# A fused eight-layer kernel without its setup block: the loads move into the first attention

## The chip, the cores and the metric

The kernel runs on one core of a Trainium2 chip as one program. The metric is the device time of a run in microseconds. Engines in the text: TensorE (PE, matrix products), VectorE (DVE), ScalarE (ACT), GpSimd (POOL) and SyncE (SP). SP issues most transfers, ScalarE some; each of the two has a queue of its own, and both queues are served by the core's 16 DMA engines.

## The reference, cut to what matters

The input is `x`, 128 sequences of 64 rows by 128 columns in float32, with a context of 128 x 64 x 96. Eight layers are added onto x: four cross attentions, each followed by a feed-forward part. Each addition is scaled by the tanh of a learned gate. Only the first two layers and the weights derived ahead of time concern the change:

```python
# layer 0: cross attention of 8 heads of 64, masked, over the context
x = x + tanh(g_xattn[0]) * (attention(layernorm(x), ctx, mask) @ W_o + b_o)
# layer 1: experts weighted by a router, around one causal attention
logits = normalize(h) @ normalize(sim_matrix, axis 0) - sigmoid(gates)
# derived ahead of time from inputs:
#  sim / |sim| per column, sigmoid(gates), tanh of the 8 gates, bias rows * tanh(gate)
#  layer 3's 128 x 128 matrix from w_freq (a Fourier transform there and back)
#  layer 6's null key and value, multiplied into W_q and W_out
```

## The kernel before, in words

`x` (64 tiles of 128 rows) stays in the on-chip memory throughout, and so do all weights of the first layers. `program` (L2463) runs `setup`, then one block after another, each with a program for every engine; between blocks stands a barrier (L2498 to L2500).

`setup` (L81) is a block of its own. SP issues 28 small loads (L181), all counted on one semaphore, `ld_small`. ScalarE issues x (4 MB, L188) and then 17 larger loads (L190). TensorE, VectorE and ScalarE each wait for all 28 small loads before their first instruction, and SP waits at the end for everything. Then the derived weights are computed: VectorE squares the router's matrix, TensorE sums the columns with a matrix of ones (L213), GpSimd takes the power -1/2 (L205); the Fourier matrices go through four products, two copies and two more (L216 to L229); the null values are 16 small products (L224); VectorE scales `l3_wq`, multiplies it by the null key and reduces it (L242 to L247), and scales six bias rows by their gates (L257).

`wide_attention` (L393) is layer 0. It works in 16 units of 4 tiles of 128 rows. Products in float32 are made of three passes over high and low parts (`product3`, L348 to L350). Each tile's step on TensorE is: transposes of the probabilities (L746), the projection of the tile before (L682), attend (L672), the scores of two tiles on (L660), for t = 1 the transposes of the normalised rows of two units on (`turn`, L620), then value, key and query jobs for later tiles. VectorE has the mask and scale (L903), the maximum (L907), the subtraction (L915), the sum and reciprocal (L921, L923), the norm's moments (L296, L301) and its scaling (L310), and the addition to x (L929). GpSimd has the norm's 1/sqrt (`rstd`, L318, L320), the multiplication of the probabilities (`scale_probs`, L549; "probs" in the prediction), the split of the context (L524, L526) and its spreading (L539, L540), and the bias (L325). ScalarE copies out of the accumulators and takes the exponential.

Ahead of the loop each engine has a written-out head, in which the first unit's keys, queries and the scores of tiles 0 and 1 are made. On GpSimd the head ends with `scale_probs(0)` and the bias of groups 0 and 1; the loop begins with `scale_probs(1)`, the split of the third unit's context and the `rstd` of the third group, then `scale_probs(2)`:

```python
scale_probs(0, first, 0)
if not null:
    norm.bias(pool, 0), norm.bias(pool, 1)
```

`gated_attention` (L2033) is layer 1. Its head on TensorE is `turn(0), router(0, 0), turn_gates(0, 0), turn(1), router(1, 1)`; between the router and `turn_gates` VectorE runs a chain of some 25 tiny instructions (L2326 to L2384), with one exponential on ScalarE in it (`gate_exp`, L2268). The gates are then written to memory, and SP loads them back spread over all partitions (L2088).

Of the kernel before, what the change touches and what calls it, by code (L numbers as in the profile page):

```python
# [12 lines left out]
P = 128  # L13
# [67 lines left out]
def setup(c, d):  # L81
# [3 lines left out]
    names = []  # L85
# [33 lines left out]
    for n in ("l3_wq", "l3_wk", "l3_wv"):  # L119
# [25 lines left out]
    c.open_work(26 * 1024)  # L145
    scr = c.work[:, 0:9 * 512].rearrange("p (n w) -> p n w", w=512)
    dftc, dfts, wr, wi = (scr[:, i, 0:D] for i in range(4))
    a1, a2, cn, sn = (scr[:, 4 + i, 0:D] for i in range(4))
    nsc = scr[:, 8, 0:D]
    simsq = c.work[:, 15 * 512:15 * 512 + 16]  # L150
    simn2 = c.work[:, 15 * 512 + 16:15 * 512 + 32]
    ones = c.work[:, 15 * 512 + 128:15 * 512 + 256]
    nprod = c.work[:, 16 * 512:18 * 512].rearrange("p (h k) -> p h k", k=DH)

    loads_small, loads_x, loads_big = [], [], []
    loads_small += [(c.w["ident"][:, :], d["ident"]), (c.w["tg"][:, :], d["gates"]), (c.w["rows"][:, :, :], d["rows"]),
                    (c.w["hm4"][:, :], d["hm4"]), (c.w["nkrow"][:, :], d["nkrow"]), (c.w["nvsel"][:, :, :, :], d["nvsel"]),
                    (c.w["nvcol"][:, :], d["nvcol"]), (c.w["gncol"][:, :], d["gncol"]), (c.w["l2_bcol"][:, :], d["l2_bcol"]),
                    (c.w["l3f_b1"][:, :], d["l3f_b1"]),
                    (dftc, d["dftc"]), (dfts, d["dfts"]), (wr, d["wr"]), (wi, d["wi"]),  # L160
                    (c.w["l3f_u1"][:, :], d["l3f_u1"]), (c.w["l3f_v1"][:, :], d["l3f_v1"]),
                    (c.w["l3f_u2"][:, :, :], d["l3f_u2"]), (c.w["l3f_v2"][:, :], d["l3f_v2"]),
                    (c.w["dup"][:, :], d["dup"]), (c.w["l0f_sim"][:, :], d["sim"]), (c.w["l0f_sig"][:, :], d["gates0"]),
                    (c.w["causal"][:, :], d["causal"]), (c.w["iota16"][:, :], d["iota16"]),
                    (c.w["l2f_wr"][:, :], d["l2f_wr"]), (c.w["l2f_bias"][:, :], d["l2f_bias"]), (c.w["tri4"][:, :, :], d["tri4"]),
                    (c.w["l3_wq"], d["l3_wq"]), (c.w["l3_wo"], d["l3_wo"])]
    for n in ("l0_wq", "l0_wk", "l0_wv", "l0_wo"):
        loads_big.append((c.w[n], d[n]))
    loads_big.append((c.ctx01[0:DC, :, :].rearrange("p a b -> p (a b)"), d["ctxT"][:, 0:2 * GT]))
    loads_big += [(c.w["l0f_w"], d["l0f_w"]), (c.w["l0f_o"], d["l0f_o"])]  # L170
    for n in ("l1_wq", "l1_wk", "l1_wv", "l1_wo", "l2_wq", "l2_wk", "l2_wvz", "l2_wo", "l3_wk", "l3_wv"):
        loads_big.append((c.w[n], d[n]))

    ld_small, ld_x, ld_big = c.sem("ld_small"), c.sem("ld_x"), c.sem("ld_big")
    xv = d["x"].rearrange("(n p) c -> p n c", p=P)
    consts, chain, pe, evac, ppow, vchain = (c.sem("su_" + n) for n in ("consts", "act", "pe", "evac", "pow", "dve"))
    with nc.Block() as block:
        @block.sync
        def _(sp):
            for dst, src in loads_small:  # L180
                sp.dma_start(dst, src).then_inc(ld_small, 16)  # L181
            sp.wait_ge(ld_small, 16 * len(loads_small))
            sp.wait_ge(ld_x, 16)
            sp.wait_ge(ld_big, 16 * len(loads_big))

        @block.scalar
        def _(act):
            act.dma_start(c.w["x"][:, :, :], xv).then_inc(ld_x, 16)  # L188
            for dst, src in loads_big:
                act.dma_start(dst, src).then_inc(ld_big, 16)  # L190
            act.wait_ge(ld_small, 16 * len(loads_small))

            A.activation(c.w["tg"][:, :], c.w["tg"][:, :], ACT.Tanh).then_inc(chain, 1)
            A.activation(c.w["l0f_sig"][:, :], c.w["l0f_sig"][:, :], ACT.Exp, scale=-1.0).then_inc(chain, 1)

        @block.gpsimd
        def _(pool):
            G.memset(ones, 1.0).then_inc(consts, 1)
            G.memset(c.w["half"][:, :], -0.5).then_inc(consts, 1)
            G.memset(c.zero[:, :], 0.0)  # L200
            G.memset(c.w["eps"][:, :], LN_EPS)

            pool.wait_ge(consts, 2)
            pool.wait_ge(vchain, 2)
            G.tensor_tensor(simn2, simn2, c.w["half"][:, :], ALU.pow).then_inc(ppow, 1)  # L205

        @block.tensor
        def _(te):
            te.wait_ge(ld_small, 16 * len(loads_small))
            te.wait_ge(vchain, 1)  # L210
            te.wait_ge(consts, 1)
            pa, pb = c.ps[:, 0, :], c.ps[:, 1, :]
            T.matmul(c.ps[:, 6, 0:16], ones, simsq, start=True, stop=True).then_inc(pe, 1)  # L213

            te.wait_ge(evac, 1)
            T.matmul(pa[:, 0:D], wr, dftc, start=True, stop=False)  # L216
            T.matmul(pa[:, 0:D], wi, dfts, start=False, stop=True)
            T.matmul(pb[:, 0:D], wr, dfts, start=True, stop=False)
            T.matmul(pb[:, 0:D], wi, nsc, start=False, stop=True).then_inc(pe, 1)

            te.wait_ge(evac, 2)
            for j in range(8):
                for b in range(2):
                    last = T.matmul(c.ps[0:16, 4, b * D:(b + 1) * D], c.w["nvsel"][:, j, b, :], c.w["l3_wo"][:, j, :],  # L224
                                    start=(j == 0 and b == 0), stop=(j == 7), skip_group_check=True)
            last.then_inc(pe, 1)
            te.wait_ge(evac, 4)
            T.matmul(c.ps[:, 5, 0:D], a1, cn, start=True, stop=False)
            T.matmul(c.ps[:, 5, 0:D], a2, sn, start=False, stop=True).then_inc(pe, 1)  # L229

        @block.vector
        def _(ve):
            ve.wait_ge(ld_small, 16 * len(loads_small))
            V.tensor_tensor(simsq, c.w["l0f_sim"][:, :], c.w["l0f_sim"][:, :], ALU.mult).then_inc(vchain, 1)
            V.tensor_scalar(nsc, dftc, -1.0, None, ALU.mult).then_inc(evac, 1)
            V.tensor_scalar(c.w["nvsel"][:, :, :, :], c.w["nvsel"][:, :, :, :], c.w["nvcol"][:, 0:1], None, ALU.mult).then_inc(evac, 1)
            V.tensor_scalar(cn, dftc, 1.0 / D, None, ALU.mult).then_inc(evac, 1)
            V.tensor_scalar(sn, dfts, 1.0 / D, None, ALU.mult)
            ve.wait_ge(pe, 1)
            V.tensor_scalar(simn2, c.ps[:, 6, 0:16], 1e-24, None, ALU.max).then_inc(vchain, 1)  # L240

            V.tensor_scalar(c.w["l3_wq"], c.w["l3_wq"], c.w["gncol"][:, 0:1], None, ALU.mult).then_inc(vchain, 1)  # L242
            ve.wait_ge(vchain, 3)
            heads = c.w["l3_wq"].rearrange("p (h k) -> p h k", k=DH)
            V.tensor_tensor(nprod, heads, bc(c.w["nkrow"][:, :], 1, 2 * HP), ALU.mult).then_inc(vchain, 1)
            ve.wait_ge(vchain, 4)
            V.tensor_reduce(c.w["l3_wnull"][:, :], nprod, AX.X, ALU.add)  # L247
            ve.wait_ge(ppow, 1)
            V.tensor_tensor(c.w["l0f_sim"][:, :], c.w["l0f_sim"][:, :], simn2, ALU.mult)
            ve.wait_ge(chain, 2)  # L250

            V.tensor_scalar(c.w["l0f_sig"][:, :], c.w["l0f_sig"][:, :], 1.0, None, ALU.add).then_inc(vchain, 1)
            ve.wait_ge(vchain, 5)
            V.reciprocal(c.w["l0f_sig"][:, :], c.w["l0f_sig"][:, :])

            for row, gate in ((0, 0), (1, 1), (2, 5), (3, 2), (4, 7), (5, 3)):
                V.tensor_scalar(c.w["rows"][:, row, :], c.w["rows"][:, row, :], c.w["tg"][:, gate:gate + 1], None, ALU.mult)  # L257
            ve.wait_ge(pe, 2)
            V.tensor_copy(a1, c.ps[:, 0, 0:D])
            V.tensor_copy(a2, c.ps[:, 1, 0:D]).then_inc(evac, 1)  # L260
            ve.wait_ge(pe, 3)
            for b in range(2):
                V.tensor_copy(c.w["l3_nwo"][:, b, :], c.ps[0:16, 4, b * D:(b + 1) * D])
            ve.wait_ge(pe, 4)
            V.tensor_copy(c.w["l1f_g"][:, :], c.ps[:, 5, 0:D])

class Norm:

# [122 lines left out]
def wide_attention(c, d, layer):  # L393

    nc = c.nc
# [95 lines left out]
    with nc.Block() as block:  # L495
# [395 lines left out]
        def _(ve):  # L891
# [84 lines left out]
            if null:  # L976
                norm.scale(ve, 1, 1)
# [1609 lines left out]
```

## Time and profile before

| | us |
|---|---|
| median of 3 runs | 3279.08 (3277.92 to 3280.07) |
| the profiled execution | 3276.91 |
| its span, first to last instruction | 3275.1 |
| TensorE busy | 3015.4 (92%) |
| VectorE busy | 2212.9 (68%) |
| ScalarE busy | 1564.1 (48%) |
| GpSimd busy | 1206.4 (37%) |
| mean granted TensorE clock | 0.969 |

The busy time of an engine is the time in which it ran an instruction. The profiled execution lies 2.2 us under the median of the runs. Times in the rows below are from the start of the span.

### The profile page before, as it was taken

To read this page: it belongs to the slowest core of one execution; us is meant where nothing else is said; L and a number is where in the kernel's file an instruction comes from. 1 tells how busy PE (TensorE), PEld (TensorE's weight loads), DVE (VectorE), ACT (ScalarE), POOL (GpSimd) and SP (SyncE) were. 2 spreads that over 40 slices of the span, in tenths; PEclk is the share of its full clock that TensorE was granted. 3 is DMA by queue.
4 is the path that set the end of the run, shared out by engine and by line. 5 is a ranking of instruction groups with operands and counts; after the bars stand their busy time and mean duration, and the time that the engine had idled before them with its cause. 6 is when DMAs were issued, how large, how long until landed. Compare 5 with 4: busy or idle time off the path is not lost. (4 is left out here: it accounts for less than half of the span.)

```text
span 3275.1 us, 90989 instructions
## 1 busy us (share of the span) xinstructions
PE 3015.4 (92%) x35250; PEld 2295.4 (70%) x35250; DVE 2212.9 (68%) x6060; ACT 1564.1 (48%) x2876; POOL 1206.4 (37%) x1408
## 2 busy tenths in 40 slices
PE   3999879999997999969997999999988999999978
PEld 2888735555555788846766888888876888888864
DVE  3677656566664555568776777777767777777755
ACT  1777611111112677636664333333335666666646
POOL 3666410000001766565441000000005766766643
PEclk8999989999998999979998999999999999999989
DMA  5000046665562000011111333333320000000001
GB/s 156 12 10 10 4 132 191 184 176 159 168 193 64 12 10 10 3 47 24 26 24 51 103 102 103 102 102 101 104 81 9 9 9 10 10 7 10 10 1 52
DMA packets 109623, 212.02 MB, mean 65 GB/s; under 512 B 18736, under 2 KB 28912, under 8 KB 108944
## 3 DMA queue, kind: packets, MB, share of 16 engines
q1 hardware_dynamic: 105232, 200.32, 21.0%
q10 hardware_dynamic: 4224, 9.59, 1.0%
q8 instruction: 91, 1.49, 0.2%
q14 instruction: 76, 0.62, 0.1%
HBM read 198.31 MB, written 5.77 MB: 62 GB/s over the span
## 5 line engine op out<-in xcount | busy, mean ns | idle before, releaser
L348 PE MATMUL ps<-parts 128*128 128x512 f32 (+2 forms) x1568 | 640.7, 409 | 46.4 <-DVE parts L953 27.6
L349 PE MATMUL ps<-parts 128*128 128x512 f32 (+2 forms) x1568 | 565.8, 361 | 0.0
L350 PE MATMUL ps<-parts 128*128 128x512 f32 (+2 forms) x1568 | 563.0, 359 | 0.0
L318 POOL TENSOR_TENSOR rstd<-mv,eps 128x4 f32<-128x4 f32 x112 | 23.8, 213 | 1223.4 <-DVE mv L301 1223.4
L348 PEld LDWEIGHTS ps<-parts 128*128 128x128 f32 (+1 forms) x1568 | 299.1, 191 | 184.9 <-ACT work L804 99.8
L1852 ACT ACTIVATE work<-ps 128x512 f32<-128x512 f32 x272 | 162.5, 597 | 453.5 <-PE ps L350 453.4
L549 POOL TENSOR_TENSOR work<-work 128x512 f32<-128x512 f32 x256 | 267.0, 1043 | 194.5 <-DVE work L923 192.6
L350 PEld LDWEIGHTS ps<-parts 128*128 128x128 f32 (+1 forms) x1568 | 298.9, 191 | 46.1
L349 PEld LDWEIGHTS ps<-parts 128*128 128x128 f32 (+1 forms) x1568 | 300.9, 192 | 13.5
L1818 PEld LDWEIGHTS ps<-early,work 128*128 128x128 f32 x2176 | 281.7, 191 | 29.8 <-DVE work L1909 11.4
L1818 PE MATMUL ps<-early,work 128*128 128x128 f32 x2176 | 289.4, 276 | 8.2 <-DVE x L2016 8.1
L1899 DVE TENSOR_TENSOR work<-work,ps 128x512 f32<-128x512 f32 x272 | 185.8, 683 | 134.2 <-PE ps L1818 120.9
L921 DVE TENSOR_REDUCE work<-work 128x8 f32<-128x512 f32 (+1 forms) x256 | 174.9, 683 | 143.5 <-ACT work L821 143.5
L2170 PE MATMUL ps<-work,early 128*128 128x512 f32 x512 | 249.4, 610 | 12.1 <-DVE work L2391 12.1
L903 DVE SCALAR_TENSOR_TENSOR ps<-ps,work 128x512 f32<-128x512 f32 x192 | 133.9, 697 | 164.6 <-PE ps L660 155.4
L804 ACT ACTIVATE work<-ps 128x512 f32<-128x512 f32 x256 | 152.8, 597 | 173.7 <-PE ps L350 170.7
L863 ACT ACTIVATE work<-ps 128x512 f32<-128x512 f32 x256 | 152.9, 597 | 133.7 <-PE ps L672 132.6
L907 DVE TENSOR_REDUCE work<-ps 128x8 f32<-128x512 f32 x256 | 176.5, 689 | 51.6 <-PE ps L660 45.0
L672 PE MATMUL ps<-work 64*64 64x64 f32 x8192 | 179.1, 225 | 20.1 <-ACT work L854 19.8
L821 ACT ACTIVATE work<-work 128x512 f32<-128x512 f32 (+1 forms) x256 | 161.9, 632 | 54.1 <-DVE work L915 52.1
L1909 DVE TENSOR_TENSOR work<-work 128x512 f32<-128x512 f32 x256 | 177.2, 692 | 15.2 <-DMA work<-expert_rows 2.6
L672 PEld LDWEIGHTS ps<-work 64*64 64x64 f32 x8192 | 145.5, 135 | 55.8 <-issue 33.6
(311 smaller groups left out, 6205.4 us busy)
## 6 DMA issues: line engine op xcount, KB each, us to landing
work<-gate_rows SPq DMA_DIRECT2D x128, 512.0 KB, 5.5
work<-expert_rows SPq DMA_DIRECT2D x512, 128.0 KB, 2.9
work<-gate_rows SPq DMA_DIRECT2D x128, 256.0 KB, 7.7
work<-in_ctxT SPq DMA_DIRECT2D x72, 192.0 KB, 2.4
out<-x SPq DMA_DIRECT2D x16, 256.0 KB, 2.3
work<-work SPq DMA_DIRECT2D x224, 16.0 KB
work<-work SPq DMA_DIRECT2D x16, 128.0 KB, 2.7
early<-in_l0f_w ACTq DMA_DIRECT2D x1, 1536.0 KB, 11.9
```

Of the source, the lines that this page charges most:

```text
L348: T.matmul(out, lh, rh, start=True, stop=False)
L349: T.matmul(out, lh, rl, start=False, stop=False)
L350: return T.matmul(out, ll, rh, start=False, stop=True)
L549: G.tensor_tensor(pn[t % 2], pr[t % 2][:, :, 0:S], bc(rec[t % 2], 2, S), ALU.mult).then_inc(p_ready, 1)
L672: last = T.matmul(ps_o[e * DH:e * DH + DH, b, j, :], vp[t % 2][rows, e, j, :], ptT[rows, j, b * S:b * S + S], start=True, stop=True)
L907: V.tensor_reduce(mx[t % 2], ps_s, AX.X, ALU.max).then_inc(max_ready, 1)
L921: V.tensor_reduce(den[t % 2], pr[t % 2], AX.X, ALU.add).then_inc(sum_ready, 1)
L1818: last = T.matmul(acc[:, t * D:(t + 1) * D], aT[b][:, t * P:(t + 1) * P], c.w["l2f_d"][:, j, :], start=(j == 0 and t == 0), stop=(j == NB ...
L1852: A.activation(sg[b], ps_g[b], ACT.Silu).then_inc(silu_ready, 1)
L1899: out = V.tensor_tensor(aT[b], sg[b], ps_u[b], ALU.mult)
L1909: V.tensor_tensor(aT[b], aT[b], wb[j % WR], ALU.mult).then_inc(a_ready, 1)
L2170: T.matmul(ps_q[u], c.w["l0f_w"][:, at:at + P], hw[p % NHW][:, e, :], start=(p == 0 and e == 0), stop=(p == NP - 1 and e == 1))
```

## The change

`setup` now only places the tensors and makes an object `Boot`, whose methods are called from the programs of layer 0's engines; there is no setup block any more. Each load has a semaphore of its own or one of a small group. The Fourier matrices come as one host-made array `dft` of five (cos, sin, -cos, cos/128, sin/128), loaded at the start of layer 1 into a buffer that is used later there, and `wri` holds the two frequency weights.

```diff
+    def sync_first(self, sp):       # SP's queue, ahead of the mask and the third context
+        sp.dma_start(*self.rows_of(0, TG)).then_inc(self.x0, 16)
+        sp.dma_start(c.ctx01[0:DC, :, :]..., d["ctxT"][:, 0:2 * GT]).then_inc(self.ctx, 16)
+        sp.dma_start(c.w["ident"][:, :], d["ident"]).then_inc(self.ident, 16)
+        sp.dma_start(c.w["l0f_sim"][:, :], d["sim"]).then_inc(self.gates, 16)
+        sp.dma_start(c.w["l0f_sig"][:, :], d["gates0"]).then_inc(self.gates, 16)
+        sp.dma_start(c.w["tg"][:, :], d["gates"]).then_inc(self.tg, 16)
+        sp.dma_start(*self.rows_of(TG, 2 * TG)).then_inc(self.x1, 16)
+    def sync_second(self, sp):      # behind them
+        sp.dma_start(c.w["rows"][:, :, :], d["rows"]).then_inc(self.rows, 16)
+        sp.dma_start(*self.rows_of(2 * TG, 4 * TG)).then_inc(self.x2, 16)
+        sp.dma_start(*self.rows_of(4 * TG, n)).then_inc(self.xr, 16)
+    def sync_third(self, sp):       # after the loads of the first two units: 6 + 25 loads
+        for dst, src in self.nulls: sp.dma_start(dst, src).then_inc(self.null, 16)
+        for dst, src in self.others: sp.dma_start(dst, src).then_inc(self.rest, 16)
+    def sync_last(self, sp):        # end of SP's program
+        sp.wait_ge(self.rest, 16 * len(self.others))
+    def scalar(self, act):          # ahead of ScalarE's first copy
+        for n, s in (("wk", self.wk), ("wq", self.wq), ("wv", self.wv), ("wo", self.wo)):
+            act.dma_start(c.w["l0_" + n], d["l0_" + n]).then_inc(s, 16)
+        act.wait_ge(self.tg, 16);    A.activation(tg, tg, ACT.Tanh).then_inc(self.tanh, 1)
+        act.wait_ge(self.gates, 32); A.activation(l0f_sig, l0f_sig, ACT.Exp, scale=-1.0)...
+    def pool_first(self, pool):     # four memsets
+    def pool_power(self, pool):     # after scale_probs(0)
+        pool.wait_ge(self.clipped, 1)
+        G.tensor_tensor(simn2, simn2, half, ALU.pow).then_inc(self.power, 1)
+    def tensor(self, te, out):      # one product of 16 columns ahead of the first key job
+        te.wait_ge(self.consts, 1); te.wait_ge(self.squares, 1)
+        T.matmul(out, ones, simsq, start=True, stop=True).then_inc(self.simn, 1)
+    def vector_first(self, ve):     # ahead of the first moments
+        ve.wait_ge(self.gates, 32); V.tensor_tensor(simsq, l0f_sim, l0f_sim, ALU.mult)...
+    def vector_second(self, ve, out):   # after shift(1), the last of VectorE's head
+        ve.wait_ge(self.simn, 1); V.tensor_scalar(simn2, out, 1e-24, None, ALU.max)  # clipped
+        ve.wait_ge(self.exp, 1);  V.tensor_scalar(l0f_sig, l0f_sig, 1.0, None, ALU.add)
+        ve.wait_ge(self.rows, 16); ve.wait_ge(self.tanh, 1)
+        for row, gate in (...6 pairs...): V.tensor_scalar(rows[row], rows[row], tg[gate], ...mult)
+        last.then_inc(self.rows_ready, 1)
+        ve.wait_ge(self.sig, 1); V.reciprocal(l0f_sig, l0f_sig)
+    def vector_last(self, ve, scratch): # ahead of VectorE's last add of layer 0
+        l0f_sim *= simn2 (power); nvsel *= nvcol (null, 6 loads); l3_wq *= gncol
+        prod = l3_wq * nkrow; l3_wnull = reduce(prod)
@@ wide_attention
 (GpSimd)  scale_probs(0, first, 0)
+          if boot: boot.pool_power(pool); pool.wait_ge(boot.rows_ready, 1)
           norm.bias(pool, 0), norm.bias(pool, 1)
+(TensorE) te.wait_ge(boot.ident, 16); te.wait_ge(boot.wo, 16); boot.tensor(te, ...)  # at its start
+(TensorE) te.wait_ge(boot.clipped, 1)      # between scores(1) and the loop
+(ScalarE) boot.scalar(act); act.wait_ge(boot.ctx, 16)  # then wk, wq, wv before their copies
+(VectorE) boot.vector_first(ve); ve.wait_ge(boot.x0, 16)  # x1 before moments(1)
+(VectorE) boot.vector_second(ve, ...); ve.wait_ge(boot.x2, 16)  # before the loop; xr in it
@@ gated_attention
+(SP)      sp.dma_start(dft, d["dft"]); sp.dma_start(wri, d["wri"])      # first of all
-            turn(0), router(0, 0), turn_gates(0, 0), turn(1), router(1, 1)
+            turn(0), router(0, 0), spectrum(), null_values(), turn_gates(0, 0), spectral_weight(), turn(1), router(1, 1)
-            take_hT(0, 0), squares(0), gate_exp(0), take_gates(0, 0)
-            take_hT(1, 1), squares(1), gate_exp(1), take_gates(1, 1)
+            take_hT(0, 0), squares(0)
+            act.wait_ge(freq_full, 1);  A.activation(freq, c.ps[:, 4, 0:2 * P], ACT.Copy)
+            act.wait_ge(nv_full, 1);    A.activation(l3_nwo, c.ps[0:16, 7, 0:2 * D], ACT.Copy)
+            gate_exp(0), take_gates(0, 0)
+            take_hT(1, 1)
+            act.wait_ge(spec_full, 1);  A.activation(c.w["l1f_g"][:, :], c.ps[:, 6, 0:P], ACT.Copy)
+            squares(1), gate_exp(1), take_gates(1, 1)
```

`spectrum` is four products of 128 columns, `null_values` the 16 small ones of setup, `spectral_weight` two of 128 columns. TensorE waits for the copies of the null values and of the spectral weight before the second pair of experts. The same instructions of setup are otherwise kept, without the negation and the two scalings of the cosine and sine matrices.

## Rows read from the trace of the kernel before

**Rows 1.** Windows: length, busy us of each engine, then PEclk, DMA share, GB/s

```profile
10.00:22.00 12.00, 0.00 (x0) 0.00 (x0) 0.00 (x0) 0.00 (x0) 0.00 (x0) 1.00 1.09 288
...
46.30:83.70 37.40, 21.69 (x194) 16.49 (x195) 19.72 (x53) 15.31 (x27) 23.48 (x24) 0.73 0.07 21
83.70:402.60 318.90, 307.76 (x5451) 258.22 (x5449) 223.66 (x510) 222.06 (x391) 202.42 (x199) 1.00 0.03 9
...
408.60:432.50 23.90, 7.03 (x29) 5.37 (x29) 10.86 (x53) 5.03 (x20) 5.32 (x10) 0.54 0.20 59
```

**Rows 2.** Waits, first 60 us: waiter, releaser: us in total, times, longest

```profile
DVE work L234 <- DMA l_wo<-in_l_wo: 38.3, 1, 38.3
```

**Rows 3.** Timeline, start of the attention: start us, us, instruction, idle before

```profile
46.31 0.63 ACT L828 ACTIVATE parts<-ctx 96x512 fp32r<-96x512 f32 x1 [7.70 <-PEq L177]
...
49.40 4.51 DVE L310 TENSOR_SCALAR work<-x,mv,rstd 128x128 f32<-128x128 f32 x4 [1.19 <-POOL rstd L320]
...
54.65 0.77 PE L348 MATMUL ps<-parts 96*128 96x512 f32 x1 [8.95 <-DVE parts L953]
```

**Rows 4.** DMA issues, first 60 us: KB each, us to landing

```profile
mask<-in_mask SPq DMA_DIRECT2D x1, 512.0 KB, 3.8
rows<-in_rows SPq DMA_DIRECT2D x1, 384.0 KB, 6.3
...
work<-in_ctxT SPq DMA_DIRECT2D x1, 192.0 KB, 3.9
...
tg<-in_gates SPq DMA_DIRECT2D x1, 4.0 KB, 2.4
```

**Rows 5.** Timeline, the attention's head into its loop

```profile
76.45 2.50 POOL L325 TENSOR_TENSOR x<-x,rows 128x512 f32<-128x512 f32 x2
76.50 0.69 DVE L915 TENSOR_TENSOR work<-ps,work 128x512 f32<-128x512 f32 x1
...
76.65 1.09 PE L746 MATMUL ps<-ident,work 128*128 128x128 f32 x4 [1.68 <-POOL work L549]
...
83.72 0.60 PE L746 MATMUL ps<-ident,work 128*128 128x128 f32 x4
...
83.90 1.12 DVE L310 TENSOR_SCALAR work<-x,mv,rstd 128x128 f32<-128x128 f32 x4 [1.18 <-POOL rstd L320]
...
86.23 0.66 PE L620 MATMUL ps<-ident,work 128*128 128x128 f32 x4
...
89.09 0.60 PE L746 MATMUL ps<-ident,work 128*128 128x128 f32 x4
```

**Rows 6.** Timeline, setup's arithmetic

```profile
39.00 0.77 PE L216 MATMUL ps<-work 128*128 128x128 f32 x2
...
39.29 0.74 DVE L242 TENSOR_SCALAR l_wq<-l_wq,gncol 128x1024 f32<-128x1024 f32 x1
...
39.52 3.28 POOL L205 TENSOR_TENSOR work<-work,half 128x16 f32<-128x16 f32 x1 [38.05 <-DVE work L240]
...
40.07 1.23 DVE L245 TENSOR_TENSOR work<-l_wq,nkrow 128x1024 f32<-128x1024 f32 x1
...
40.98 4.08 PE L224 MATMUL ps<-l_wo,nvsel 128*16 128x128 f32 x32
...
43.30 1.17 DVE L257 TENSOR_SCALAR rows<-rows,tg 128x128 f32<-128x128 f32 x6
```

**Rows 7.** Timeline, the end of the attention

```profile
401.55 1.04 POOL L549 TENSOR_TENSOR work<-work 128x512 f32<-128x512 f32 x1 [3.63 <-DVE work L923]
...
406.74 0.75 DVE L929 SCALAR_TENSOR_TENSOR x<-ps,tg,x 128x512 f32<-128x512 f32 x1 [5.26 <-PE ps L682]
```

**Rows 8.** Timeline, the opening of the second stage

```profile
414.32 1.89 PE L2152 MATMUL ps<-l0f_sim,work 128*128 128x16 f32 x8 [0.69 <-ACT work L2257]
...
422.27 0.26 ACT L2268 ACTIVATE work<-work 128x64 f32<-128x64 f32 x1 [6.41 <-DVE work L2374]
```

**Rows 9.** Timeline, ScalarE's issue of the first weight behind x

```profile
1.69 14.93 ACTq L190 DMA_DIRECT2D early<-in_l_wq  x1
```

More of the change, by code:

```diff
@@ L144, in setup @@
     res("tri4", [P, 4, 4])
[L145 to L166, printed above, removed]
@@ L176, in setup @@
[L176 to L265, printed above, removed]
@@ L513, in _ @@
             body(0, False)
+            if boot:
+                boot.sync_third(sp)
             if n > 3:
@@ L576, in _ @@
             scale_probs(0, first, 0)
+            if boot:
+                boot.pool_power(pool)
+                pool.wait_ge(boot.rows_ready, 1)
             if not null:
@@ L693, in project @@
                     last.then_inc(acc_ready, 1)
+            if boot:
+                te.wait_ge(boot.ident, 16)
+                te.wait_ge(boot.wo, 16)
+                boot.tensor(te, c.ps[:, 7, 0:NE0])
             te.wait_ge(low, 1)
@@ L726, in _ @@
             scores(1, first, 1)
+            if boot:
+                te.wait_ge(boot.clipped, 1)
             te.wait_ge(q_done, NJ + 2)
@@ L984, in body @@
                         beyond = isinstance(it, int) and it >= c.ngroup - 2
+                        if boot and isinstance(it, int) and it == 0 and u == 1 and t == 3:
+                            ve.wait_ge(boot.xr, 16)
                         if not null and not last and t == 1:
@@ L1019, in _ @@
             else:
+                if boot:
+                    boot.vector_last(ve, kT[0].rearrange("p j q -> p (j q)")[:, 0:2 * HP * DH])
                 add(c.ngroup - 1)
@@ L2053, in gated_attention @@
     cnt, m1, m2, km = w([TG]), w([TG]), w([TG]), w([TG])
+    dft, wri, freq = mixed[0].rearrange("p a b -> p (a b)")[:, 0:5 * P].rearrange("p (n w) -> p n w", w=P), sm[:, 0:2, :], sm[:, 2:4, :]
+    dft_in, freq_full, freq_out, spec_full, spec_out, nv_full, nv_out = (
+        c.sem("f0_" + x) for x in ("dft_in", "freq", "freq_out", "spec", "spec_out", "nv", "nv_out"))
     ps_q, ps_v = [c.ps[:, i, :] for i in range(2)], [c.ps[:, 2 + i, :] for i in range(2)]
@@ L2217, in back, with spectrum, spectral_weight, null_values @@
                     last.then_inc(y_ready, 1)
-            turn(0), router(0, 0), turn_gates(0, 0), turn(1), router(1, 1)
+            def spectrum():
+                te.wait_ge(dft_in, 32)
+                for out, terms in ((c.ps[:, 4, 0:P], (0, 1)), (c.ps[:, 4, P:2 * P], (1, 2))):
+                    for i in range(2):
+                        last = T.matmul(out, wri[:, i, :], dft[:, terms[i], :], start=(i == 0), stop=(i == 1))
+                last.then_inc(freq_full, 1)
+            def spectral_weight():
+                te.wait_ge(freq_out, 1)
+                for i in range(2):
+                    last = T.matmul(c.ps[:, 6, 0:P], freq[:, i, :], dft[:, 3 + i, :], start=(i == 0), stop=(i == 1))
+                last.then_inc(spec_full, 1)
+            def null_values():
+                for j in range(8):
+                    for b in range(2):
+                        last = T.matmul(c.ps[0:16, 7, b * D:(b + 1) * D], c.w["nvsel"][:, j, b, :], c.w["l3_wo"][:, j, :],
+                                        start=(j == 0 and b == 0), stop=(j == 7), skip_group_check=True)
+                last.then_inc(nv_full, 1)
+            turn(0), router(0, 0), spectrum(), null_values(), turn_gates(0, 0), spectral_weight(), turn(1), router(1, 1)
             for p in range(NP):
+                if p == 1:
+                    te.wait_ge(nv_out, 1)
+                    te.wait_ge(spec_out, 1)
                 project(0, 0, p)
```

128 lines of the change are left out of this document (114 added, 14 removed).

## The prediction

> **What bounds the kernel now.** I read the windows table first, because it tells which stretches are idle and which are full. TensorE works 308 of the 319 us from 83.7 to 402.6 us, the body of the first attention, at the full granted clock; the change adds nothing inside that body's steady loop, so there is nothing to gain or lose there but a delay that enters at its head. From 10 to 22 us no engine computes and the DMA engines are full at 288 GB/s; from 46.3 to 83.7 us TensorE works 21.7 of 37.4 us at a mean clock of 0.73, a chain of dependent small steps; the opening of the second stage (408.6 to 432.5 us) is a chain as well, TensorE 7 of 24 us [rows 1]. Then the waits: VectorE's first instruction waits 38.3 us for the last small load, as the setup block waits for all of its 28 small loads at once [rows 2]. What follows is 8 us of setup arithmetic, and the first attention starts at 46.3 us [rows 3]. All of that stands on the path: the loads and the arithmetic of setup run beside nothing.
>
> **The change, step by step. Start of the attention.** The attention's first instructions (ScalarE's copy of the context, VectorE's moments) now wait only for what they read. On SP's queue ahead of the gates `tg`, the sixth DMA, stand x0 (256 KB), the context (384 KB), ident (64 KB) and two tables of 8 KB: 0.72 MB. On ScalarE's queue stand the four weights, 896 KB. Together 1.62 MB. SP's issues come each 0.45 to 0.48 us, so the sixth is issued at about 3.1 us. For the rate there are two rows: 288 GB/s with two full queues [rows 1], and the 704 KB of mask and context that the attention loads on an idle machine, which have landed 3.8 and 3.9 us after their issues, 4.3 us after the first [rows 4]. From that row, 0.9 MB more at 288 GB/s is 3.2 us: 0.7 + 4.3 + 3.2 = 8.2 us for all six and the weights. Then tanh and exp, two short ScalarE instructions (gate_exp, of 64 columns, takes 0.26 [rows 8], these have 8 and 16), 0.5 us with their waits, and 0.1 for the semaphore: ScalarE's copy starts at 8.8 us instead of 46.3. VectorE's path is one of the two tables ahead of it, then the squares (0.2 us) and the moments, so it starts no later. The table load of 1.3 us falls in the time of the loads. Gain 37.5 us.
>
> Bounds of that start. From below: a small load on a quiet queue has landed 2.4 us after its issue [rows 4], so 5.5 us + 0.5 = 6 us. From above: in the kernel before, SP's queue beside ScalarE's 4 MB of x moved `rows` (384 KB) in 6.3 us [rows 4], 4 of them after the first byte: a queue may get only some 80 to 100 GB/s. At that rate 0.72 MB are 9 us, but the other queue now holds 0.9 MB and not 4, which at the remaining 200 GB/s are gone in 4.5 us. So 13 us is the far end.
>
> The Trainium skill ("DMA: Bandwidth & Descriptors", Queues, rings and completion order) has each DMA engine alternate between queue rows packet by packet, which would give SP's big-row packets a fair half; `rows` in 6.3 us disagrees with a fair half of 288 GB/s (2.7 us for 384 KB). By the page's rule alone SP's 0.72 MB would take 5 us and the start would fall at 8.3; nothing here changes by it.
>
> What the transfers left behind do: x1, mask, next context, rows, x2 and xr (together 4.9 MB at 288 GB/s, 17 us) are gone by about 25 us. Their first users come, on the shifted clock, at 17 us (x1: 8.7 us after the start), 29 us (mask), 39 us (rows, x2). x1 is next in the queue behind `tg` and lands a microsecond after it. Nothing waits. The 31 loads of sync_third (5.6 MB by the shapes, 20 us) are issued during the second unit; one unit lasts 4 tiles of 5.0 us (318.9 us for 64 [rows 1]), 20 us. The context load of the sixth unit is due when they end, waits at most 5 us behind their last, and is needed a unit after it: 20 us of cover. Zero.
>
> **Head of the attention: what is added before the loop.** On the clock of before, VectorE ends shift(1) at 77.2 us [rows 5]; the new clip of simn2 ends at 77.4. TensorE, which transposed tile 0 at 76.65 [rows 5], now first waits for `clipped`: +0.85 us. The larger term is GpSimd's. Its queue is probs(0) (ends 76.5), bias (2.50 us), probs(1), split, rstd, and VectorE's norm scale at 83.90 waits for that rstd [rows 5]. The power of 128x16, 3.28 us [rows 6], now stands ahead of the bias and starts at 77.45, 0.95 us after GpSimd came free. So all behind it is late by 0.95 + 3.28 = 4.2 us: probs(1) ends at 84.2 (TensorE wants it at 83.72 + 0.85 = 84.6: hidden), the norm scale runs from 88.1 to 89.3, and TensorE's turn(2), at 86.23 before [rows 5], now waits for it until 89.4. That is +3.2 us, and contains the 0.85. VectorE's sums(2) and GpSimd's probs(2) follow at 90.2 and 91.3, and TensorE asks for them at 89.1 + 3.2 = 92.3: hidden. In the body GpSimd works 202 of 319 us [rows 1], so it catches up. VectorE's own additions (the six row scalings 1.2 us [rows 6], two small ones and the reciprocal, together under 2 us) end at 79.2, before GpSimd is at probs(1). Cost 3.2 us. Least 0.85, if GpSimd's delay is absorbed. Most: all of 4.2, 1.2 for the rows and 2 to 3 us of TensorE at the low clock for longer, since it stands idle around turn(2): 8 us.
>
> On the 1.2 us: in setup a two-input VectorE instruction of 128x1024 took 1.23 us beside that same power on GpSimd [rows 6], 1.2 ns a column like the 0.69 us for 512 columns at 76.50 [rows 5], so the power held it up by less than 0.1 us. The Trainium skill ("SBUF — State Buffer", Who interferes with whom) calls the port pair of VectorE and GpSimd an exclusive lock for the whole instruction, taken by tensor_scalar too. By this rule the six row scalings would stand until the power ends and the bias, which now waits for rows_ready, would begin 1.2 us later: 4.4 us instead of 3.2. The row speaks against it for tensor_tensor; for tensor_scalar nothing shows it with a power, and I keep 3.2.
>
> **Tail.** vector_last stands ahead of VectorE's last add, for which it idles 5.26 us before 406.74 [rows 7]. Its work: 0.3 (nvsel, a quarter of l3_wq's size, and l0f_sim) + 0.74 + 1.23 + 1.23 (the reduction, taken like the product of the same size) = 3.5 us [rows 6]. Four tensor_scalar beside GpSimd's splits took 4.51 us and four without 1.12 [rows 3, 5], so it may not start before GpSimd's last probs end at 402.6 [rows 7]: done at 406.1, hidden with 0.6 to spare; if VectorE goes first, GpSimd's probs and TensorE behind them lose 0.4. I take 0.2; most 1.5.
>
> **Opening of the second stage.** TensorE gets 4 small products (about 2.0 us, 39.00 to 40.98) and 16 null products (4.08 us) [rows 6] between router(0), which ends at 416.2, and turn_gates(0) [rows 8]: done at 422.3. Their loads (448 KB from 408.6) have landed by then, by the 4.3 us for 704 KB. But ScalarE now copies the null values (256 columns, 0.4 us) before gate_exp, which ran at 422.27 [rows 8]: now 422.8. +0.5 us, passed on to the rows sent out and spread again. The third product and the copies after it fall in TensorE's and ScalarE's idle time. Between 0 and 2.
>
> **Sum.** -37.5 + 3.2 + 0.2 + 0.5 = -33.6 us. The profiled execution took 3276.9 us (span 3275.1): 3243.3. The median of the runs is 2.2 above it: 3245.5, rounded to 3246. My own range for this case is 3239 to 3253.
>
> **Rivals.**
> (a) Late data: ScalarE's queue or SP's starves the other, as `rows` hints, and the start falls at 13 to 20 us. For it: wq's issue took 14.9 us behind x [rows 9]. Against it: here x's big remainder, xr, stands last in its queue. At 18 us: 9 less gained, 3255. Chance 0.10.
> (b) Head cost larger: GpSimd's delay keeps TensorE in gaps, the clock stays at the low of its two levels (1.2 GHz; the mean of 0.73 in the head [rows 1] is a mix of the two) for some tiles more. 3251 to 3256. Chance 0.10.
> (c) Nothing lost: power and bias hidden, start at 7 us: 3279.1 - 39.3 + 1 = 3241 or a little under. Chance 0.08.
> (d) Slower than before. One mechanism: the delays at the head leave TensorE in gaps in every tile, so that its clock does not come back. The four transposes of a tile took 1.09 us in the low stretch and 0.60 after it [rows 5], 1.8 times; TensorE's 5.0 us of a tile would be up to 9.0. At 4 us a tile the 9th slow tile eats the gain of 34; with 12, 3246 + 48 = 3294. Against it: before, the transposes of tile 1 are back at 0.60 after idle places of the same kind, and stay there [rows 5]. Chance 0.03.
> (e) The change does not do what it says: the gates are held up on the queue until x is in, as if a block still stood there (start at 25 us, 3262): 0.03.
> The forecast has the remaining 0.66. The time can be told from no change beyond 0.2%, 6.6 us. Faster by more than that: all but (d) and a trace of unknowns, 0.95; within it 0.02; slower 0.03. Range for 8 in 10: 3239 to 3255, which takes in (b), half of (c) and a part of (a).
>
> **What would show it.** ScalarE's first copy at 8.8 us (6 to 13). First product of key_job 8.3 us after it. The power on GpSimd for 3.3 us between probs(0) and the bias, and the first turn in the loop 3.2 us later, counted from the start of the attention, with TensorE waiting there for VectorE's norm scale. Attention from its start to its last add 364.6 us instead of 361.2. gate_exp half a microsecond later after the stage's start. A start after 13 us, a low clock after the second tile, or a wait for a DMA inside the attention would make the prediction wrong.

## The result, and the profile after

The changed kernel takes 3247.9 us (median of 4 runs, 3244.8 to 3251.1), the kernel before 3278.6 beside it (3277.9 to 3280.1): a ratio of 0.990 (0.989 to 0.991), 31 us less. The forecast was 3246, within 3239 to 3255. The profiled execution took 3244.8 us (span 3243.0), where the sum was 3243.3.

I cut both spans at the start of the attention (VectorE's first moments) and at the start of each stage's last add. All numbers are us:

```
                        before   after   difference
start of the attention    46.3     9.4     -36.9
first attention          360.4   363.1      +2.7
second stage             629.5   629.2      -0.3
next attention           354.8   354.6      -0.2
narrow attention, its MLP 366.3  368.4      +2.1
next spectral stage      691.5   692.3      +0.8
next attention           732.8   732.5      -0.3
last stage                89.5    89.5       0.0
span                    3275.1  3243.0     -32.1
```

The lengths are differences of places rounded to 0.1 us, so their last digit can be off by one.

The windows of after, for the stretches of [rows 1] moved by the 37 us (the same columns):

```profile
9.30:46.70 37.40, 21.34 (x194) 16.36 (x195) 21.30 (x63) 15.22 (x28) 22.96 (x22) 0.92 0.44 123
46.70:368.40 321.70, 310.67 (x5454) 260.41 (x5452) 224.65 (x513) 222.55 (x391) 205.91 (x202) 0.99 0.09 27
374.50:398.40 23.90, 13.83 (x73) 11.31 (x74) 11.32 (x54) 5.84 (x23) 5.14 (x10) 0.65 0.26 89
```

The head has the same 194 matmuls in the same 37.4 us, now with the DMA engines busy for 0.44 of it instead of 0.07: the loads run beside the arithmetic. The opening of the second stage has 73 matmuls where it had 29: setup's products stand there.

The start: the wait that releases VectorE, then the two tables' and the large transfers' issues, then the timeline.

```profile
DVE simsq L233 <- DMA l0f_sig<-in_gates: 9.3, 1, 9.3
```

```profile
ctx<-in_ctxT SPq DMA_DIRECT2D x1, 384.0 KB, 5.8
rows<-in_rows SPq DMA_DIRECT2D x1, 384.0 KB, 7.8
...
l0f_sig<-in_gates SPq DMA_DIRECT2D x1, 8.0 KB, 6.5
tg<-in_gates SPq DMA_DIRECT2D x1, 4.0 KB, 6.2
```

```profile
9.26 0.18 DVE L233 TENSOR_TENSOR simsq<-l0f_sim 128x16 f32<-128x16 f32 x1 [9.26 <-DMA l0f_sig<-in_gates]
...
9.71 0.61 ACT L844 ACTIVATE parts<-ctx 96x512 fp32r<-96x512 f32 x1
...
12.40 4.51 DVE L304 TENSOR_SCALAR work<-x,mv,rstd 128x128 f32<-128x128 f32 x4 [1.19 <-POOL rstd L314]
...
17.66 0.77 PE L342 MATMUL ps<-parts 96*128 96x512 f32 x1 [7.50 <-DVE parts L975]
```

The 38.3 us of [rows 2] are 9.3. Both engines wait for tables of 4 and 8 KB that land 6.2 and 6.5 us after their issue, behind 0.7 MB. From the first moments to the first product it is 8.3 us, as in [rows 3]: the chain is moved and not changed.

The head into the loop, which answers to [rows 5] (start, us, instruction, idle before it and its releaser). Its last two lines are the norm scale of the third group of rows and that group's transposes on TensorE, `turn(2)`, the first turn inside the loop:

```profile
40.06 1.29 DVE L244 TENSOR_SCALAR rows<-rows,tg 128x128 f32<-128x128 f32 x6
...
40.08 2.90 POOL L222 TENSOR_TENSOR simn<-simn,half 128x16 f32<-128x16 f32 x1
...
42.95 2.51 POOL L319 TENSOR_TENSOR x<-x,rows 128x512 f32<-128x512 f32 x2
...
47.93 1.05 PE L759 MATMUL ps<-ident,work 128*128 128x128 f32 x4
...
50.41 1.11 DVE L304 TENSOR_SCALAR work<-x,mv,rstd 128x128 f32<-128x128 f32 x4 [4.19 <-POOL rstd L314]
...
51.71 0.66 PE L627 MATMUL ps<-ident,work 128*128 128x128 f32 x4
```

The power stands between probs(0) and the bias, and VectorE's norm scale waits 4.19 us for the rstd behind it (1.18 in [rows 5]). But TensorE's turn(2) at 51.71 has no wait: TensorE is late by itself. The windows show a low clock there (columns as in [rows 1]):

```profile
33.40:41.40 8.00, 3.25 (x42) 2.20 (x42) 4.66 (x15) 3.00 (x6) 7.40 (x7) 0.94 0.01 2
41.40:49.40 8.00, 7.39 (x83) 6.59 (x84) 4.05 (x15) 3.15 (x6) 7.84 (x8) 0.50 0.00 1
```

TensorE worked 3.25 of 8 us, and in the next 8 us its granted clock is 0.50, the level of 1.2 GHz; four transposes took 1.05 us there instead of 0.60 [rows 5].

The tail and the opening of the second stage, which answer to [rows 7, 8]:

```profile
367.26 1.13 POOL L551 TENSOR_TENSOR work<-work 128x512 f32<-128x512 f32 x1 [3.63 <-DVE work L945]
...
367.40 1.54 DVE L255 TENSOR_SCALAR l_wq<-l_wq,gncol 128x1024 f32<-128x1024 f32 x1
...
370.23 1.22 DVE L260 TENSOR_REDUCE l_wnull<-work 128x16 f32<-128x1024 f32 x1
...
372.53 0.75 DVE L951 SCALAR_TENSOR_TENSOR x<-ps,tg,x 128x512 f32<-128x512 f32 x1 [1.08 <-PE ps L689]
...
380.23 1.89 PE L2191 MATMUL ps<-l0f_sim,work 128*128 128x16 f32 x8 [0.69 <-ACT work L2319]
...
383.94 4.24 PE L2274 MATMUL ps<-l_wo,nvsel 128*16 128x128 f32 x32
...
388.21 0.37 ACT L2360 ACTIVATE l_nwo<-ps 16x256 f32<-16x256 f32 x1 [3.79 <-PE ps L2274]
...
388.49 0.24 ACT L2330 ACTIVATE work<-work 128x64 f32<-128x64 f32 x1
...
389.77 0.61 PE L2199 MATMUL ps<-ident,work 128*16 128x128 f32 x4 [1.59 <-DVE work L2454]
```

Setup's last VectorE work fits into the idle time before the last add: 1.08 us of it are left. In the second stage gate_exp (L2330) starts 13.94 us after the stage's (13.62 before), held by the null values' copy, and yet the stage is no longer.

### The profile page after: what moved, and what is told of

The parts are those of the page before. It is cut to its first block and busy times, and to the rows that moved or that the text cites. A ratio compares the mean times of both kernels' runs of the same rounds, so it can differ in the third digit from the quotient of the medians.

```text
span 3243.0 us, 90979 instructions
## 1 busy us (share of the span) xinstructions
PE 3020.5 (93%) x35250; PEld 2299.3 (71%) x35250; DVE 2210.6 (68%) x6052; ACT 1564.5 (48%) x2878; POOL 1207.0 (37%) x1408
```

## The experiments

The theory: the loads' overlap gives the 37 us, and of the 2.7 lost again in the attention the power's place in GpSimd's queue is the cause. Rivals: the clock's chance makes the 2.7; the start is set by the bytes shared between the queues and not by the order of the tables; the work put into the second stage costs what the narrow attention shows. The expectations give them letters of their own. Runs of one session ran on one chip; positions in the head are counted from VectorE's first moments. Every run below has one profile, and the places and stage lengths given for it are that one execution's.

**First session.** The changed kernel again, and three other placements.

e0, the changed kernel itself:

> The changed kernel itself, timed beside the others on one chip. Its four first runs spread from 3244.8 to 3251.1 us, the kernel before only from 3277.9 to 3280.1. Theory 1 (the spread is the chip's, in the stages after the second): median 3247 to 3249, ratio to before 0.989 to 0.991, attention from VectorE's first moment to the end of the last add 364.0 us again. Theory 2 (the moved loads or the new head make the time vary): the first attention's length differs from 364.0 by more than 1 us.

3249.5 us (3246.5 to 3253.2; before there 3281.4): 0.991 (0.989 to 0.992). Here TensorE does wait for the norm scale:

```profile
50.98 1.12 DVE L304 TENSOR_SCALAR work<-x,mv,rstd 128x128 f32<-128x128 f32 x4 [4.32 <-POOL rstd L314]
...
52.15 0.66 PE L627 MATMUL ps<-ident,work 128*128 128x128 f32 x4 [2.07 <-DVE work L304]
```

Turn(2) falls at 42.6 after the start (42.4 in after, 39.9 before), and the attention takes 365.3 us. So two reasons come to the same place: GpSimd's queue, in both, and the low clock, in after. TensorE waits there in e5, e6 and e10 below too (2.07, 1.34 and 2.02 us), which all have the power in this place: in four of the five profiles of this placement, not in the first. Where it waits for 2 us, the way from turn(2) to the first addition to x takes 15.6 to 15.7 us instead of some 14.3.

e1, the power behind a later bias:

```
             if boot:
-                boot.pool_power(pool)
                 pool.wait_ge(boot.rows_ready, 1)
 ...
                             if t == 2:
                                 norm.bias(pool, un.k + 2)
+                                if boot and it == 0 and u == 0:
+                                    boot.pool_power(pool)
```

> GpSimd's power is moved from the head into the first unit of the loop, behind the bias of its third tile, where GpSimd idles 2.6 us; all else as changed. Theory A (the 2.9 us of the power ahead of bias, probs(1), split and rstd are the cost of the head): VectorE's norm scale of the third group comes 2.9 us sooner, turn(2) 2.4 us sooner, the attention takes 361.3 to 362.0 us from its first moment to its last add instead of 364.0; whole time 2 to 2.7 us below the changed kernel. Theory B (the cost is TensorE's wait for the clip and its low clock after it): norm scale sooner, but turn(2) less than 1 us sooner and the attention 363.2 or more.

3247.5 us (3242.8 to 3248.3). Turn(2) comes 1.6 us sooner than in e0 (2.4 expected) and the attention is 361.9 us. The whole is 2.0 us shorter than e0, which the spread of the runs doesn't let one tell from nothing. The bias now waits for the scaled rows, so not all of the power's 2.9 us came back:

```profile
41.96 2.51 POOL L319 TENSOR_TENSOR x<-x,rows 128x512 f32<-128x512 f32 x2 [1.28 <-DVE rows L244]
...
49.43 1.11 DVE L304 TENSOR_SCALAR work<-x,mv,rstd 128x128 f32<-128x128 f32 x4 [2.88 <-POOL rstd L314]
```

e2, both additions at an idle place of the head:

```
             spread(first, 0)
+            if boot:
+                boot.pool_power(pool)
             split_rows(0, 0)
 ...
             weights_low(2, wvl, wvh, wv, DC)
+            if boot:
+                boot.vector_second(ve, c.ps[:, 7, 0:NE0])
             ve.wait_ge(ht_full, 1)
```

> All of VectorE's second part (clip, gates, six rows, reciprocal) is moved ahead of its 9.8 us wait for the second rstd, and GpSimd's power into its 8.3 us wait for the high rows; no setup work is left between the head and the loop. Theory A: attention 361.2 to 361.8 us, like e1 and at most 0.8 less (TensorE's wait for the clip goes too); whole time 2.5 to 3.3 below the changed kernel. Theory B: attention 361.2, but e1 363.2 or more. Theory C (the low clock after the head comes from the shorter start and not from the moved work): attention stays above 363 in both.

3248.5 us (3245.2 to 3249.4). The norm scale stands at 38.2 (37.6 before, 41.4 in e0), turn(2) at 40.8, the attention is 362.2 us. With e1 this points at 1 to 3 us of the attention for the placement of the power (after and e0 363.1 and 365.3; e1 and e2 361.9 and 362.2), but e3, next, has e2's placement and 365.4. In the whole time it can't be told from the spread of the runs.

e3, e2 and SP's first DMAs in the order sim, gates0, tg, x0, context, ident:

> As e2, and SP issues the router matrix, its gates and tg first, then x0, context, ident. Theory L (the start is set by the bytes queued ahead of the tables): VectorE's squares start at 3.5 to 4.5 us instead of 9.3, the first moment when x0 lands, near 7, ScalarE's first copy when the context lands, near 8; start of the attention 1 to 2.5 us sooner than e2, whole time lower by the same. Rival R (the two queues share by bytes, so what is ahead on one queue hardly matters and all lands at 8 to 9): start less than 0.7 us sooner.

```profile
3.76 0.17 DVE L233 TENSOR_TENSOR simsq<-l0f_sim 128x16 f32<-128x16 f32 x1 [3.76 <-DMA l0f_sig<-in_gates]
...
9.00 0.87 DVE L290 BATCH_NORM_STATS2 st<-x 128x6 f32<-128x128 f32 x4 [5.06 <-DMA x<-in_x]
...
10.72 0.63 ACT L845 ACTIVATE parts<-ctx 96x512 fp32r<-96x512 f32 x1 [4.86 <-DMA ctx<-in_ctxT]
```

The tables land 5.5 us sooner, x0 and the context take their place as the last to come, and the start moves by 0.35 us against after (0.4 against e2), as the rival has it. ScalarE's first copy even stands 1.0 us later than in after. 3246.4 us (3242.1 to 3247.1), no gain that can be told.

Its attention takes 365.4 us, as long as e0's, though no setup work stands between its head and the loop. Two things make that up. The four transposes of tiles 0 and 1 take 1.09 and 1.05 us, those of the low clock, and turn(2) is at 41.7 (40.8 in e2). And from the second to the third addition to x, where the last loads end, it takes 23.9 us; the same step is 21.0 in before, b0, after, e1 and e10, 21.2 in e6, 21.5 in e0, e2 and e4, 22.3 in e5, 22.4 in e7 and 24.8 in e8 (in e9 the step before it is longer, 21.9 instead of 20.9). From there to the last addition all the profiles agree within 0.4 us. What the placement of the power changes is thus read at turn(2) and not from the attention's length: 42.4 to 42.6 in all five profiles with the power in its first place, 40.8 to 41.7 in e1, e2 and e3, 39.9 and 42.1 in the two of the kernel before.

**Second session.** b0, the kernel before, profiled a second time:

> The kernel before, profiled a second time. Four profiles of the changed kernels have 368.4 to 368.9 us from the end of the second attention to the last add of the narrow attention, the one of before 366.3; it loses 2.4 us in a stage that the change doesn't touch, with TensorE's clock at 0.91 in five of the first nine stretches of 20 us of its loop instead of none of five. Theory S (the clock of that stage falls where it will, run by run): here 366 to 369, not 366.3 again. Theory T (the change, by its shift of the start or of addresses, sets it): 366.3 within 0.3.

3279.1 us. Its start falls at 47.6, 1.3 us later than in the first profile. It has the low clock in the head too, though no power stands there, and its turn(2) is at 42.1, not at 39.9:

```profile
86.14 1.05 PE L746 MATMUL ps<-ident,work 128*128 128x128 f32 x4
...
89.75 0.66 PE L620 MATMUL ps<-ident,work 128*128 128x128 f32 x4
```

Its attention took 362.7 us (360.4 in the first). So a part of what I called the power's price is the chance of the clock: over both profiles each, 361.6 before and 364.2 after.

e5, the changed kernel with both first engines also waiting for the rest of x:

```
+        act.wait_ge(self.xr, 16)
         act.wait_ge(self.tg, 16)
 ...
+                ve.wait_ge(boot.xr, 16)
                 boot.vector_first(ve)
```

> The changed kernel, but VectorE and ScalarE wait before their first work for the last part of x (xr, landed at 25.6 us in the changed kernel), as the old block waited for its loads. Theory W (the gain is the wait for data that nobody needs yet): first moment at 25.7 to 26.5 us instead of 9.4, the whole 16 to 17 us longer, 3261 to 3266. Of the 37 us of the gain 16 to 17 are then xr's, some 12 the later loads' and 8 the arithmetic's. Rival: the head would be as fast with its data in place and part of the delay is taken back: less than 14 us longer.

The start falls at 25.7, 16.3 us late, as expected; the whole is 3272.1 us, 6 to 11 above what I expected. Against e0, of another session (25.6 more in the profiled executions), 16.1 us are the start, 0.8 the attention and 8.6 the stages behind it; why those, this one execution can't settle. Of the start it is shown that the loads running beside the first chain make some 16 of its 37 us; the rest is the other loads and the block's arithmetic, which this run left out of the path too.

e6, without the work put into the second stage (spectrum, null values and spectral weight are left out of the computation, zeros stand for them):

> Leaves out the spectral weight and the null values in the second stage (their loads, 22 products and three copies; both are set to zero), all else as changed. As predicted it cost +0.5 us; the trace shows gate_exp 0.3 us later but turn_gates' transposes 0.6 instead of 1.0 us and the first experts' products 0.7 us earlier. Theory G (the extra products keep TensorE's clock up and pay for themselves): gate_exp 0.3 us sooner from the stage's start, the transposes 1.0 us again, the first experts' product 0.3 to 0.7 us LATER from the stage's start. Rival: without the work the stage's head is 0.3 to 0.5 us shorter.

```profile
388.67 0.26 ACT L2327 ACTIVATE work<-work 128x64 f32<-128x64 f32 x1 [6.42 <-DVE work L2435]
...
389.97 1.02 PE L2199 MATMUL ps<-ident,work 128*16 128x128 f32 x4 [7.37 <-DVE work L2445]
```

3245.5 us (3241.4 to 3249.4), second stage 629.3 us. Without the extra products gate_exp comes 0.3 us sooner (13.64 after the stage's start), but TensorE has stood idle for 7.4 us and its four transposes take 1.02 us. In after they take 0.61, behind products that fill the idle time, and the routing rows are out at 16.47 against 16.61 here; the first experts' product starts at 23.13 after the stage's start against 23.68 here. The extra products win back by the clock what the copy costs.

e7, e2 and 20 useless products in TensorE's idle places of the head (10 behind turn(1), 10 behind scores(1)):

```
                 turn(1)
+                if boot:
+                    te.wait_ge(boot.clipped, 1)
+                    for i in range(10):
+                        T.matmul(c.ps[:, 7, :], kh[0:DC, 0:P], kh[0:DC, :], start=True, stop=True)
```

> As e2_head_early, with twice 10 products of 128x512 on TensorE in the two idle places of the head (their results are overwritten), each run 2.3 us at the full clock in gaps of 2.7 us. Theory K (what is left of the head's cost is the low clock that the gaps leave, 0.50 from 41 to 47 us): the clock stays at 1.00 through the head, the attention takes 359.5 to 361 us instead of 362.2, whole time 1 to 2.5 us below e2. Rival: the fillers delay the query jobs and the first transposes by as much: 362 or more.

```profile
33.40:41.40 8.00, 6.59 (x58) 4.46 (x56) 4.00 (x9) 3.19 (x6) 7.67 (x8) 1.00 0.01 2
41.40:49.40 8.00, 7.05 (x160) 6.11 (x161) 5.11 (x19) 4.33 (x8) 5.71 (x7) 1.00 0.10 28
```

The clock stays up and turn(2) comes 1.7 us sooner than in e2 (39.1). The attention gets 0.8 us of that (361.4); the other 0.9 go in the step where the last loads end (22.4 us instead of 21.5), not in the head; 3246.1 us (3244.6 to 3246.4).

**Third session.** e4: the low part of the key weights ahead of the first norm scale on VectorE, with e1's power and e2's vector_second:

```
             V.tensor_tensor(cl[0][0:DC, :], c.ctx01[0:DC, 0, :], ...).then_inc(low, 1)
+            if boot:
+                weights_low(0, kl, kh, wk, DC)
             norm.scale(ve, 0)
```

> As e2 (but with the power in the loop, as in e1), and on VectorE the low part of the key weights, which the first product waits for, stands ahead of the first norm scale instead of behind it: that scale takes 4.5 us beside GpSimd's splits. Theory P (the first 8.3 us of the attention are this queue order): first product at 12.1 to 12.6 us instead of 17.7, turn(0) 5 us sooner, the attention 357 to 359 us, whole time 3 to 5 below e2, 3243 to 3246. Rival Q (the next link, GpSimd's spread and the split of the high rows, binds as soon): turn(0) sooner, but the first query job less than 2 us sooner, attention 360.5 or more.

```profile
11.30 0.68 DVE L976 TENSOR_TENSOR parts<-early,parts 96x512 fp32r<-96x512 f32 x1
...
12.12 0.76 PE L342 MATMUL ps<-parts 96*128 96x512 f32 x1 [1.79 <-DVE parts L976]
...
12.89 4.57 DVE L304 TENSOR_SCALAR work<-x,mv,rstd 128x128 f32<-128x128 f32 x4 [0.91 <-POOL rstd L314]
...
17.51 0.66 PE L628 MATMUL ps<-ident,work 128*128 128x128 f32 x4 [0.68 <-DVE work L304]
```

The first product stands 2.6 us after the start instead of 8.3, because it no longer waits behind 4.5 us of norm scale. Turn(2) is at 36.0 (41.0 in e1), the attention is 357.3 us. 3240.9 us (3238.7 to 3241.7; before there 3279.6): 0.988 (0.987 to 0.990), the shortest median of all the kernels run, and below both kernels. Of the 6.5 us below e1's median, which is of another session, the attention explains 4.6.

e8, e4 with e7's products:

> e4 with the filler products of e7. If the low clock costs what e7 shows (0.8 us against e2, turn(2) 0.5 us or more sooner), the attention is 0.5 to 1.5 us shorter than e4's. Rival: the gaps of the head have shrunk with e4 and the fillers now cost: longer than e4's.

3241.8 us (3237.5 to 3242.8), no better. Its turn(2) comes 2.2 us sooner than e4's and its attention is 1.2 us longer. The time goes after the head: a stop of TensorE without a releaser, where the last loads end, and a lower clock behind it. That e4's single profile had a short stop (0.16 us) and e8's a long one is chance as far as these runs tell, so they don't say what the products are worth.

```profile
86.36 0.34 PE L680 MATMUL ps<-work 64*64 64x64 f32 x7 [2.10 <-issue]
```

```profile
63.10:83.10 20.00, 20.00 (x349) 16.63 (x339) 14.37 (x34) 13.88 (x26) 14.19 (x14) 1.00 1.01 287
83.10:103.10 20.00, 17.41 (x271) 14.75 (x271) 11.04 (x22) 12.33 (x22) 9.61 (x11) 0.91 0.07 16
```

e9, e8 and the load of wo moved from ScalarE's queue to SP's, behind `rows`, with TensorE's wait for it moved to the end of the head:

> e8 with the output weights (256 KB) moved from ScalarE's queue to SP's, behind the bias rows, and TensorE's wait for them to the end of the head. Theory L2 (the start is set by all bytes in flight ahead of the tables, 1.6 MB): 256 KB less is 0.9 us at 288 GB/s, squares at 8.3 to 8.6 us instead of 9.3. Rival: wo is last on its queue and its packets come mostly after the tables: less than 0.3 us.

The start moves by 0.3 us, to 9.0, where all bytes in flight would have given 0.7 to 1.0: 256 KB fewer on the other queue hardly help SP's. Its turn(2) is at 36.1, 2.2 us later than e8's: the first products come 0.43 us apart until 24.2 us, in e8 only until 15.9. 3241.8 us (3239.9 to 3243.6).

e10, the changed kernel with the 31 loads of sync_third issued at once, not in the loop:

> The changed kernel with the 31 loads of sync_third issued directly behind sync_second, so that the DMA engines are full until some 45 us and not 25. I costed these loads at nothing wherever they stand. Prediction's theory: no wait for a DMA in the attention beyond the head's; turn(2) within 0.5 us of the changed kernel's place from the start, attention 363 to 365.5. Rival: the loads delay the next contexts or the fetching of instructions: a wait for a context load in the first units, attention over 367.

3247.4 us, a single run. No engine waits for a DMA in the attention, turn(2) is at 42.5, the attention is 364.6 us: this placement of the burst costs nothing that one run can show, and TensorE does not stop in the loop.

## Why the prediction was right

**Start: -37.5 expected, -37.0 measured.** ScalarE's copy starts at 9.7, not at 8.8; the gates, not the big transfers, come last. My sum had all six DMAs of SP and the weights landing together at 8.2. Only a part of its model is borne out. e3 shows that the order on SP's queue hardly moves the start, as it should be if the bytes ahead of all the first users count. But e9 takes 256 KB of the other queue away and gets 0.3 us, not the 0.9 that the sum gives them. So the sum came within 0.9 us of ScalarE's copy, partly by luck: how the two queues share stays open. Rival (a), late data, did not happen: the start stands below 13 us in every run without an added wait. Rival (e) fell with it.

**Head: +3.2 expected.** The mechanism is right: the power between probs(0) and the bias (2.90 us, not 3.28) shifts the norm scale by 3.5 us (4.2 expected) and turn(2) by 2.5 in after, 2.7 in e0; e1 and e2 take a part of it away. They bring turn(2) to 41.0 and 40.8, not to 39.9, and b0, which has no power there, is at 42.1: against both profiles of before, the shift of turn(2) in after is 1.4 us. That TensorE waits there for VectorE holds in e0, e5, e6 and e10; in after and in b0 it is late by the clock, and the two reasons do not add. The attention came out 2.7 us longer in the first pair of profiles, 2.6 over two pairs, where 3.2 + 0.2 was the sum; which part of it is the power's and which the clock's can be told only roughly from single profiles. I took the first profile's 0.60 us for tile 1's transposes as the kernel's; it was that execution's. Rival (b) has its mechanism here, but not its size: the low clock ends at about 50.6 us, 4 us into the loop, with tile 2's transposes back at 0.60 us. Rival (d) did not occur: the clock is 0.99 over the loop.

The six row scalings started beside the power and took 1.29 us. An exclusive hold of the port pair, as the Trainium skill ("SBUF — State Buffer", Who interferes with whom) describes it for tensor_scalar in the modes that use both ports, would have kept them until the power ended at 42.98. If these six ran in such a mode, which no row tells, the trace disagrees for this operation. Beside GpSimd's work on the context and the rows the picture is another: four norm scales still take 4.51 us, and the six row scalings 2.85 in e8. Why the power is different no run shows.

**Tail: +0.2 expected, +0.1 measured.** It ran as described, with a margin of 1.08 us. VectorE did go beside GpSimd's last probs: 1.54 us instead of 0.74 for one and 1.13 instead of 1.04 for the other.

**Opening of the second stage: +0.5 expected.** gate_exp is 0.3 us late, and the step that failed is "passed on to the rows": e6 shows that the rows are not late, since TensorE's clock is up. Term: 0.

**Elsewhere: nothing expected, +2.1 in the narrow attention and its MLP.** Nothing of the change stands there. The whole stage, before and after, in windows of the two kernels (columns as in [rows 1]):

```profile
1390.98:1757.33 366.35, 313.85 (x4612) 233.38 (x4612) 275.13 (x709) 214.74 (x358) 175.87 (x205) 0.93 0.11 28
```

```profile
1356.26:1724.68 368.42, 317.42 (x4612) 236.46 (x4612) 274.93 (x709) 214.67 (x358) 175.88 (x205) 0.92 0.11 27
```

The same 4612 matmuls take TensorE 3.6 us more, at a granted clock of 0.92 instead of 0.93; the busy times of VectorE, ScalarE and GpSimd are the same within 0.2 us. The stage's length over all profiles goes from 364.3 (b0) to 368.9, with changed kernels at 364.5 (e6), 365.7 (e4) and 365.8 (e10) too. It varies from execution to execution. That most changed kernels lie at the long end (nine of them at 368.4 to 368.9) is not explained. In the first pair of profiles, which gained 32.1 us where the sum had 33.6, these 2.1 us are more than the whole difference: without them the other terms would have come out 0.6 us better than the sum. The medians are 31 us apart.

## What to carry to other kernels

A setup block that waits for all its loads costs the sum of the loads; let each engine wait for what it reads, and the loads run beside the first chain of small steps. Put the freed work by looking at what is queued behind it on its own engine: 2.9 us of a power on GpSimd put TensorE's next turn at 42.4 to 42.6 us of the attention at one place and at 40.8 to 41.7 at others. Then look at the chain that has become first: a single reordering on VectorE, by which the first product no longer waits behind 4.5 us of other work, gave more than all the placements of setup's work together.

## What was not expected of the hardware

A small table is no cheaper than its place: 4 and 8 KB landed 6.2 to 6.5 us after their issue behind 0.7 MB, 2.4 us on a quieter queue [rows 4].

TensorE stopped with no releaser where the full DMA burst of some 20 us ends: 2.10 us in e8, 1.26 in e3, 0.99 in e7, 0.98 in e5, 0.64 in e9, 0.16 in e0, e2 and e4, and not at all in after, e1, e6 and e10, which has no burst there. With the lower clock behind it this made the step of 21.0 us up to 3.7 us longer, so the 31 late loads, which the prediction put at nothing, cost nothing in after but did cost in other executions. That TensorE fetched code late behind the transfers is a guess; no run tested it. The traces fit it: in all eight profiles with a stop, TensorE goes on 1.2 to 1.5 us after a 16 KB packet of the DMA queue that the profile calls `instruction` has ended. Whose code that packet held they don't tell.

The granted clock's column reads 1.00 from after's first product to 33 us, while the key products (96x512) come 0.43 us apart until 22.5 us and 0.23 us apart from 23.8 us on. The old kernel's first key products are 0.43 us apart as well, from 54.7 to 58.6 us, and there its column reads 0.50. After's windows over the two stretches:

```profile
17.40:22.50 5.10, 4.84 (x12) 3.78 (x13) 2.45 (x12) 1.79 (x3) 0.00 (x0) 1.00 1.06 291
22.50:33.00 10.50, 7.97 (x66) 5.59 (x64) 2.88 (x8) 6.01 (x11) 4.38 (x5) 1.00 0.21 57
```

Both read 1.00, though only the second has the narrow spacing: at the start of a kernel I would go by the spacing.
